# Reading every expert's tile count from one packed word, and writing the eight experts out on TensorE

## The reference, cut to what matters

```python
E, TOPK, I = 8, 2, 938
out = swiglu(x, shared_gate_up, shared_down)          # every token
probs = softmax(x @ gate_weight.T)
top_p, sel = top_k(probs, TOPK)                       # two experts a token
top_p = top_p / (sum(top_p) + 1e-8)
cw = sum(top_p[..., None] * one_hot(sel, E))
for e in range(E):
    out = out + cw[..., e:e + 1] * swiglu(x, experts_gate_up[e], experts_down[e])
```

## Time and profile before

| | |
|---|---|
| median of 3 runs | 829.33 us (828.41 to 831.73) |
| profiled execution | 833.42 us |
| its span | 831.6 us |
| TensorE busy | 690.9 us, 83% of the span |
| VectorE busy | 572.3 us, 69% |
| ScalarE busy | 424.7 us, 51% |
| GpSimd busy | 381.5 us, 46% |
| mean granted TensorE clock | 0.911 |

### The profile page before, as it was taken

One profiled execution on the slowest core, in us unless ns is written; L12 is line 12 of the kernel. 1 busy time (PEld: TensorE's weight loads), 2 busy tenths in 40 slices (PEclk: granted clock), 3 DMA queues, 4 the chain that ended last, 5 costly groups with the idle time before them and its releaser, 6 DMA issues.

```text
span 831.6 us, 11904 instructions
## 1 busy us (share of the span) xinstructions
PE 690.9 (83%) x3134; PEld 529.0 (64%) x3135; DVE 572.3 (69%) x1227; ACT 424.7 (51%) x821; POOL 381.5 (46%) x300
## 2 busy tenths in 40 slices
PE   3736889988888899887877998999989999999920
PEld 1425666756666676665645877777778777887710
DVE  3666888878788888888553665566656665666637
ACT  2413757475574757464433555555555555555510
POOL 2462264554446374555232745547228145632236
PEclk9758899999899999999787999999999999999975
DMA  7302000000000001000041203030303003000036
GB/s 236 88 1 70 20 27 25 26 25 19 6 32 19 25 26 25 26 25 27 7 162 62 95 24 108 12 108 24 98 23 94 26 16 108 25 25 27 28 108 205
DMA packets 38202, 44.37 MB, mean 53 GB/s; under 512 B 5334, under 2 KB 28880, under 8 KB 38184
## 3 DMA queue, kind: packets, MB, share of 16 engines
q1 hardware_dynamic: 33576, 35.69, 13.9%
q0 software_dynamic: 4608, 8.47, 3.1%
HBM read 31.42 MB, written 13.76 MB: 54 GB/s over the span
## 4 chain that ended last, share of the span: by engine, by line
PE 58%; DVE 22%; issue 8%; ACT 4%; DMA 2%; SPq 2%; POOL 2%; another core or an unknown queue 1%; DVEq 1%; ACTq 0%; POOLq 0%
PE PS L576 54%; PE PS L579 4%; DVE prod L1189 2%; DVE acc L1207 2%; DVE diag L1284 1%; DVE delta L1228 1%; DVE wd L1280 1%; DVE X L1308 1%; ACT L1021 1%; DVE r L1346 1%; DVE oh L1349 1%; DVE al L1194 1%; DVE stats_a L1174 1%; DVE r L1347 1%
## 5 line engine op out<-in xcount | busy, mean ns | idle before, releaser
L916 ACT ACTIVATE sg<-PS 128x512 f32<-128x512 f32 x216 | 129.3, 598 | 208.3 <-PE PS L576 179.0
L576 PE MATMUL PS<-xh,w_lo 128*128 128x512 f32 x432 | 188.6, 437 | 21.7 <-DVE prod L1189 10.5
L1189 DVE TENSOR_TENSOR PS<-PS,sg 128x512 f32<-128x512 f32 x160 | 111.9, 699 | 131.0 <-PE PS L576 111.1
L576 PE MATMUL PS<-xh,w_hi 128*128 128x512 f32 x432 | 172.8, 400 | 0.0
L576 PE MATMUL PS<-xl,w_hi 128*128 128x512 f32 x432 | 172.8, 400 | 0.0
L535 POOL DMA_INDIRECT result_dram<-y_rows,aux_d x80 | 78.0, 975 | 200.6 <-DVE y_rows L1540 161.8
L576 PEld LDWEIGHTS PS<-xh,w_lo 128*128 128x128 f32 x432 | 83.8, 194 | 52.5 <-issue 18.3
L469 POOL DMA_INDIRECT sorted_dram<-h,slot x64 | 71.3, 1115 | 93.3 <-DVE slot L1384 66.3
L1194 DVE TENSOR_TENSOR al<-PS,ah 128x512 fp32r<-128x512 f32 x160 | 109.2, 683 | 6.4 <-ACT ah L923 3.9
L923 ACT CAST ah<-PS 128x512 fp32r<-128x512 f32 x160 | 93.2, 582 | 15.2 <-DVE PS L1189 13.5
L576 PE MATMUL PS<-ah,w_lo 128*128 128x512 f32 x216 | 93.7, 434 | 4.0 <-ACT ah L923 4.0
(11 more groups left out here) (218 smaller groups left out, 1136.1 us busy)
## 6 DMA issues: line engine op xcount, KB each, us to landing
stage<-in_w_gu SPq DMA_DIRECT2D x18, 469.0 KB
xin<-sorted_dram SPq DMA_DIRECT2D x20, 260.0 KB, 2.6
stage<-in_w_dn SPq DMA_DIRECT2D x9, 448.0 KB
tab<-mods_dram SPq DMA_DIRECT2D x8, 384.0 KB, 3.5
sorted_dram<-pad SPq DMA_DIRECT2D x8, 260.0 KB
out<-X SPq DMA_DIRECT2D x4, 512.0 KB, 3.2
stage<-result_dram SPq DMA_DIRECT2D x3, 512.0 KB, 5.1
result_dram<-y_rows,aux_d POOLq DMA_INDIRECT x80
```

The source lines that it names most:

```text
L576: return nc.tensor.matmul(out, lhsT, rhs, start=start, stop=stop, **k)
L916: A.activation(sg[:, c % 3, :], bank("gate", where, c), ACT.Silu).then_inc(s["silu_done"], 1)
L1189: V.tensor_tensor(product_in(where, c), bank("up", where, c), sg[:, c % 3, :], ALU.mult).then_inc(s["prod_done"], 1)
```

## The change

TensorE no longer loads counts and first tiles expert by expert. VectorE packs the eight counts less one as the digits of one number to the base 8 (at most 8^8 - 1) and stores it as one integer, `word`. A constant row with the powers of 8 is added to `small`. TensorE waits for it, loads it once, and gets each count by a shift, a mask and an addition. It keeps the running number of tiles in a register. The eight experts are written out without the loop over pairs, so `tile_body` is written eight times.

```diff
+MAX_TILES = TOKENS // TILE
...
-    small = np.concatenate([upto, equal, block, *roles, seg, E - expert, expert * REGION, many], 1)
+    digit = MAX_TILES ** np.arange(E)[None, :] + 0 * u
+    small = np.concatenate([upto, equal, block, *roles, seg, E - expert, expert * REGION, many, digit], 1)
...
+        word_f = sb("word_f", [P, 1])
+        word = sb("word", [P, 1], I32)
...
-            def expert(e, buf, first=None):
-                if first is None:
-                    tiles, first = tiles_of(pe, e)
-                else:
-                    tiles = tile_count(pe, e)
+            pe.wait_ge(s["word_ready"], 1)
+            digits = pe.value_load(word[0:1, 0:1], min_val=0, max_val=MAX_TILES ** E - 1)
+            bits = MAX_TILES.bit_length() - 1
+            count = 0
+            for e in range(E):
+                tiles = pe.snap(((digits >> bits * e) & MAX_TILES - 1) + 1, min_val=1, max_val=MAX_TILES)
                 pe.wait_ge(s["split_done"], e + 2)
                 apart(pe)
                 with pe.Fori(0, tiles) as t:
-                    tile_body(buf, first + t)
-                return first + tiles
-
-            with pe.Fori(0, E // 2 - 1) as k:
-                expert(2 * k + 1, 0, expert(2 * k, 1))
-            count = expert(E - 1, 0, expert(E - 2, 1))
+                    tile_body((e + 1) % 2, count + t)
+                count = pe.snap(count + tiles, min_val=1, max_val=MAX_FIRST)
...
             V.tensor_copy(plan[:, 0:2, :], plan_f[:, 0:2, :]).then_inc(s["plan_ready"], 1)
             V.engine_nop().then_inc(s["aux_read"], 1)
+            link(V.scalar_tensor_tensor(plan_f[:, 3, :], plan_f[:, 0, :], -1.0, S["digit"], ALU.add, ALU.mult))
+            link(V.tensor_reduce(word_f[:], plan_f[:, 3, :], AX.X, ALU.add))
+            V.tensor_copy(word[:], word_f[:]).then_inc(s["word_ready"], 1)
```

More of the change, by code:

```diff
@@ L101 @@
 for _name, _n in (("upto", BLK), ("equal", BLK), ("block", NB), ("upper", 9), ("lower", 9), ("seg", E * GC),
-                  ("rev", E), ("region", E), ("many", E)):
+                  ("rev", E), ("region", E), ("many", E), ("digit", E)):
     SMALL[_name] = (_at, _n)
@@ L257, in adaln_block @@
             ah_ready al_ready al_late down_done y_bank_done y_sb_ready yt_done y_out gated_free tile_in xt_done rh_ready
-            rl_ready aux_read aux_moved results_out plan_ready pads_out final_added final_gated final_sum final_ready_dve final_ready_pool
+            rl_ready aux_read aux_moved results_out plan_ready word_ready pads_out final_added final_gated final_sum final_ready_dve final_ready_pool
             out_done gb_in""".split()
@@ L272, in adaln_block @@
         NRAW = 4
-        MAX_TILES = TOKENS // TILE
         MAX_FIRST = 2 * TOKENS // TILE + E
```

## The result

The changed kernel takes 848.3 us (median of five executions, 843.8 to 849.05) where the kernel before takes 829.33, on record with five executions too. The ratio on record is 1.0214 (the two medians alone would give 1.0229), with a 95% interval of 1.0181 to 1.0246. So the change makes the kernel slower beyond the scatter; whether by more or less than 2% is not settled. The forecast was 821.0. The profiled execution took 843.8 us, the shortest of the five (before 833.42), with a span of 842.0.

The account below looks back on a forecast made before the run. TensorE was taken to bound the expert stage. Gaps -6.1, clock -1.6 and start -0.6 sum to -8.3 us, from the median of 829.33 to 821.0 us; range 817.5 to 825.5.

Parts of the forecast that it names:

- The seven gaps: TensorE between experts: seven idle gaps shrink from 9.7 us to 3.6, 6.1 us less (bounds 4.0 and 6.9).
- My first rival: Register work in TensorE's gaps is as dear as a load: 823.1 us, 824.7 if the clock still falls; chance 0.13.
- The sum for a gap: TensorE between two experts: 0.82, less 0.60 for loading, plus 0.30 of register work, gives 0.52 us (bounds 0.40 and 0.82).
- The clock: TensorE's one clock fall behind a long gap between experts disappears: 1.6 us less (bounds 0 and 3.2).
- The start: TensorE's first matmul of the expert stage follows `xh` sooner: 0.6 us less (bounds 0 and 0.65).
- VectorE's three operations: Behind `plan_ready` they delay VectorE 0.6 us, hidden under TensorE's wait for `xin`: cost 0 (bounds 0 and 0.6).
- The other engines: Engines still loading two registers between experts, ScalarE the tightest, do not hold TensorE back: cost 0 (bounds 0 and 3.5).
- The length of the code: About 720 more instructions on TensorE cost 0 (bounds 0 and 3.8), with 10 or 11 packets in the instruction queue.
- The rivals 2, 3 and 4: Gaps move to engines behind, 824.5 us, 0.08; code fetched once more, 824.8, 0.08; code refetched at branches, 838.5, 0.04.
- The fourth rival: TensorE's code is fetched at branches back, stalling every tile of two late experts: slower, 838.5 us; chance 0.04.
- The fifth: TensorE's gaps between experts stay by the writing of the loops; only clock and start gain: 827.1 us; chance 0.05.
- The signs: TensorE's profile: seven alike gaps of about 0.5 us; wrong if over 0.7 or idle time inside late experts' tiles.

Follow-up runs that it names:

- Holding both values: Changed kernel with each expert's tile count and the running number moved into registers of their own: 820.04 us, ratio 0.9895 against the kernel before.
- the run with the word unread: Kernel before with VectorE's three operations, the word and the longer constant added, TensorE left as it was: 832.45 us, ratio 0.9995.
- the held kernels: Changed kernel with values moved into registers: tile count and running number 820.04 us, running number alone 823.27, tile counts alone 825.9.
- the second chip: Chip where the changed kernel, unaltered, was run again: 849.21 us, ratio 1.0213; the kernel before had a median of 833.0 there.
- the two doses at the head: 24 or 8 register instructions added at each tile's head, to the kernel before with eight bodies and counts loaded ahead (818.5 us): 877.2 and 838.96 us.
- the large dose: 24 register instructions and a met wait added at each tile's head, to the kernel with counts loaded ahead (818.5 us): 877.2 us, ratio 1.0555.

## Why the prediction was wrong, step by step

- *The seven gaps* failed. The step said that the new count and the running number are added "with the moves of the two results into their own registers", once per expert. There were no moves. The number and the place of the operations were wrong: 69 pairs at the heads of tiles, and the bound of the loop at each tile's end, instead of four operations at each of seven ends. From expert 1 to 7 the gap inside an expert grows by (2.08 - 0.42) / 6 = 0.28 us per earlier expert, of which the pair's own rows are 0.032 + 0.113 and the rest lies outside them. Holding both values took away 22.2 - 3.6 = 18.6 us. Of that the running number has 22.2 - 6.5 = 15.7 and the bound 2.9. The 15.7 are less than 69 x 0.28 = 19.1, because a held number has to be made once at each of the seven ends: a gap between experts is 0.45 longer than one inside where it is held, and 0.1 where it is not, which is 7 x 0.35 = 2.4. The last 1.0 is not accounted for. My first rival asked what a mask costs, and no rival asked how often it is run.
- *The sum for a gap* came out once the moves were made: 0.47 to 0.55 for my 0.52, 3.6 for my 3.6, and 820.04 for the 821.0 of the whole. The 0.60 for a load stands (0.61 with the loop written out). In the 0.30 for what is added there is luck: it was four singles at 0.076, and the rows behind the first expert (at 475.1 us) show two fused ones of 0.084 and 0.093 and one single of 0.036, while a single takes 0.092 in time. Fewer operations at a higher price came to the same sum.
- *The clock* failed with it: there were five gaps of 1.76 us and more, and two to three falls instead of none. With the values held there was none behind a gap.
- *The start* was right: 0.6 us gained, `xh` to first matmul 0.04. *VectorE's three operations* were right as far as the run with the word unread can tell: no change within 0.35%, and the wait for `xin` still ends last.
- *The other engines* were right: no gap moved to them in the held kernels.
- *The length of the code* was right as to time, and the 10 or 11 packets came as 11. The Trainium skill, page "Runtime: NRT & Kernel Launch", section "Instruction fetch mechanics", would have a branch out of the window fetch its target first; the written-out kernels show no gap that such a fetch would explain, and no row tells whether one of their branches left the window. The rivals 2, 3 and 4 fall with this.
- The fourth rival had the right side, and about half of the loss (838.5), by the wrong mechanism. A kernel that is slower by a cause in each tile is what it described; the cause was register work and not code. The fifth had the gaps stay by the writing of the loops: the seven between experts did, 9.4 us of 9.7, and the eleven inside experts it did not have.
- The signs that I named were the right ones: the chain of waits has not "seven gaps between experts, all alike" but 18 unlike ones, and idle time before late tiles.

The medians differ by 19.0 us in the result and by 16.2 on the second chip; the account gives 15.8. The falls of the clock, 1.4 to 1.6 us each, vary from run to run and could hold part of the rest, and so could the end of the first part; that was not shown.

## What to carry to other kernels

A name in the program is not a register: where a loop uses a value that was computed outside it, move it into a register and look in the compiled loop for what is left. Register work counted one for one at a tile's end, at about 0.1 us an instruction, and about half of 2.3 us of it was hidden in the middle of a queue of matmuls. A plan that eight loads can fetch under a wait that is there anyway needs no packing.

## What the runs showed of the hardware

- On TensorE's sequencer a single register operation or move is 0.029 to 0.036 us in its row and 0.092 in time (the two doses at the head); a load of a register from on-chip memory 0.30 (0.49 for the first); a compare-and-branch 0.08 when it falls through (0.083 at 480.3 us in the kernel before) and 0.21 to 0.22 when it jumps (0.223 at 462.6).
- In the expert stage the granted clock fell behind idle gaps of 1.76 us or more in 12 of 34 (1 of 2 in each of three profiles of kernels with the old gaps, 3 of 5 and 2 of 5 in the two of the changed kernel, 4 of 18 with the large dose), and behind none of 1.66 or less. Behind each of the 12 the granted clock of the stretch is 0.63 to 0.67, between the two levels of 1.2 and 2.4 GHz, and each costs 1.4 to 1.6 us. With 2.3 to 2.7 us of idle time before every tile it fell less often, not more, than I had expected.
- Eleven packets of code instead of eight, and eight loops of two or three rounds instead of four written bodies, cost nothing that can be seen: with the loop over pairs written out the ratio is 0.9952.
- In the middle of a tile about 1.1 of 2.3 us of register work was hidden, at its head none.
